# Causal masks added in f32r instead of bf16 in a 24-batch attention and experts kernel

## What is computed

```
# layer 0, "mla":  latent attention, softmax
scores = einsum('bhqd,bhkd->bhqk', q, k) * scale
causal = triu(full((t, t), -inf), k=1)
attn = softmax(scores + causal)
# layer 1, "gqa":  grouped attention, 16 query heads on 4 key heads
scores = where(tril(ones(s, s)), scores, finfo.min);  attn = softmax(scores)
# layer 1, "spm":  the same with sparsemax in softmax's place
scores = where(tril(ones(l, l)), scores, -1e9);       attn = sparsemax(scores)
```

## Time and profile before

| what | value |
|---|---|
| median of 3 runs | 3103.69 us |
| lowest, highest | 3096.67, 3104.48 us |
| the profiled execution's own time | 3129.51 us |
| span in its profile, first to last instruction | 3127.6 us |
| mean granted clock of TensorE in it | 0.956 |
| busy: PE, PEld, DVE, ACT, POOL | 90%, 73%, 68%, 52%, 48% |

### The profile page before, as it was taken

How to read it: one execution, slowest core, us unless ns; L and a number is a source line. 1 busy time by engine, 2 the same in 40 slices (tenths; PEclk the granted TensorE clock), 3 DMA queues, 4 the chain that set the end, 5 groups by cost and what they waited for, 6 DMA issues and landing times. The chain is left out here.

```text
span 3127.6 us, 61182 instructions
## 1 busy us (share of the span) xinstructions
PE 2809.4 (90%) x20990; PEld 2275.6 (73%) x20990; DVE 2133.4 (68%) x6013; ACT 1615.2 (52%) x3388; POOL 1506.6 (48%) x2213
## 2 busy tenths in 40 slices
PE   5877799999999999978998898998799999999996
PEld 3555478888899889846666666666588888888864
DVE  6878678788788788767777877766644444454565
ACT  3544344444454445545655555655455555555553
POOL 4768743443343354385556666322233333332487
PEclk8878799999999999989999999999899999999998
DMA  3555578788888888422333344210466666665355
GB/s 83 197 208 202 196 262 311 278 286 316 284 290 307 294 286 308 178 40 55 97 99 104 105 107 109 93 69 22 164 213 210 228 213 212 204 241 203 124 97 126
DMA packets 212008, 580.13 MB, mean 185 GB/s; under 512 B 24617, under 2 KB 146417, under 8 KB 167409
## 3 DMA queue, kind: packets, MB, share of 16 engines
q1 hardware_dynamic: 172528, 523.82, 47.7%
q0 software_dynamic: 36864, 51.14, 8.1%
q10 hardware_dynamic: 2304, 1.21, 0.1%
HBM read 450.14 MB, written 125.96 MB: 184 GB/s over the span
## 5 line engine op out<-in xcount | busy, mean ns | idle before, releaser
L1139 POOL TENSOR_TENSOR al<-t,ah 128x512 fp32r<-128x512 f32 x220 | 283.4, 1288 | 875.1 <-ACT ah L1375 875.1
L481 PE MATMUL bank<-xh,gu 128*128 128x256 f32 x3520 | 672.3, 291 | 33.6 <-DVE gc L1654 25.8
L481 PEld LDWEIGHTS bank<-xh,gu 128*128 128x128 f32 x3520 | 512.6, 190 | 57.7 <-issue 55.0
L524 PE MATMUL bank<-masks_bf,ident_bf 128*128 128x128 bf16 x1896 | 432.9, 252 | 133.9 <-DVE st L1840 41.0
L1840 DVE TENSOR_REDUCE st<-bank 128x1 f32<-128x512 f32 (+3 forms) x1024 | 422.1, 481 | 166.1 <-PE bank L542 158.6
L1472 ACT ACTIVATE pt<-bank 128x512 f32<-128x512 f32 (+1 forms) x1152 | 512.0, 540 | 30.2 <-PE bank L545 21.9
L524 PEld LDWEIGHTS bank<-masks_bf,ident_bf 128*128 128x128 bf16 x1896 | 170.3, 99 | 353.6 <-DVE st L1840 95.3
L1480 ACT ACTIVATE oT<-bank 128x512 f32<-128x512 f32 x192 | 114.6, 597 | 602.5 <-PE bank L621 576.5
L542 PE MATMUL bank<-ksT,qsT 128*128 128x512 f32 (+3 forms) x1536 | 410.3, 369 | 5.7 <-DVE top L1838 3.1
L545 PE MATMUL bank<-qaT,ksT 128*128 128x512 f32 (+3 forms) x1536 | 399.6, 372 | 0.0
L481 PE MATMUL bank<-xl,gu 128*128 128x256 f32 x1760 | 351.5, 281 | 0.0
(11 more groups left out here) (250 smaller groups left out, 5216.2 us busy)
## 6 DMA issues: line engine op xcount, KB each, us to landing
gu<-wu_scratch SPq DMA_DIRECT2D x110, 1032.0 KB, 5.2
gu<-wu_scratch SPq DMA_DIRECT2D x110, 1024.0 KB, 7.4
dn<-wd_scratch SPq DMA_DIRECT2D x110, 1024.0 KB, 6.7
xs<-xs_scratch SPq DMA_DIRECT2D x110, 264.0 KB, 4.3
ys_scratch<-yb SPq DMA_DIRECT2D x110, 256.0 KB, 7.0
raw<-in_gu SPq DMA_DIRECT2D x16, 1024.0 KB
wu_scratch<-hi SPq DMA_DIRECT2D x16, 1024.0 KB
wu_scratch<-lo SPq DMA_DIRECT2D x16, 1024.0 KB
```

Source lines behind the costliest of these rows:

```text
L481: mm = pe.matmul(bank[:, TS * h:TS * (h + 1)], gu[:, col:col + P], x[s % 2][:, TS * k:TS * (k + 1)], start=(n == 0), stop=(n == len(terms) ...
L524: return pe.matmul(S.bank((which, G, u))[:, diag:diag + P * len(unit)], ident_bf[:, :], masks_bf[:, side, 0:len(unit), :].rearrange("p n k ...
L1139: pool.tensor_tensor(em["al"][s % 2][:, m, :], em["t"][g % 2][:, :], em["ah"][s % 2][:, m, :].bitcast(F32), ALU.subtract).then_inc(al_read ...
```

## The change

Where a mask starts the accumulation, its product is now of f32r: the identity `ident_r` and the triangles `masks_r`, both rounded to f32r once at the start, with the triangle of the unit of two blocks read twice by a broadcast. The operands take 4 bytes an element instead of 2. Where a mask comes last (the q calls within the stretches with experts, and the general pipeline), it stays as it was, with a `masks_bf` that now holds only the triangles of the q side. The masking number becomes minus 2 to the 100th, a power of two, so that rounding leaves it as it is. DVE makes four casts in place of two at the start, and TensorE waits for all four before the first scores. No instruction of TensorE is added, removed or moved.

```
-MASKED = -1.0e30
+MASKED = -2.0 ** 100
...
-    masks_bf = sb("masks_bf", [P, 2, 2, P], BF16)
+    masks_bf = sb("masks_bf", [P, 2, P], BF16)
+    masks_r = sb("masks_r", [P, 2, P], F32R)
+    ident_r = sb("ident_r", [P, P], F32R)
...
-                        return pe.matmul(S.bank((which, G, u))[:, diag:diag + P * len(unit)], ident_bf[:, :],
-                                         masks_bf[:, side, 0:len(unit), :].rearrange("p n k -> p (n k)"),
-                                         start=start, stop=not start, skip_group_check=True)
+                        to = S.bank((which, G, u))[:, diag:diag + P * len(unit)]
+                        if start:
+                            return pe.matmul(to.rearrange("p (n k) -> p n k", k=P), ident_r[:, :],
+                                             bcast(masks_r[:, side, :], 1, len(unit)), start=True, stop=False,
+                                             skip_group_check=True)
+                        return pe.matmul(to, ident_bf[:, :], masks_bf[:, 0:len(unit), :].rearrange("p n k -> p (n k)"),
+                                         start=False, stop=True, skip_group_check=True)
...
-                    pe.wait_ge(cast, 2)
+                    pe.wait_ge(cast, 4)
...
                     dve.tensor_copy(ident_bf[:, :], ident[:, :]).then_inc(cast, 1)
-                    dve.tensor_copy(masks_bf[:, :, :, :], bcast(boot["masks"][:, :, :], 2, 2)).then_inc(cast, 1)
+                    dve.tensor_copy(ident_r[:, :], ident[:, :]).then_inc(cast, 1)
+                    dve.tensor_copy(masks_r[:, :, :], boot["masks"][:, :, :]).then_inc(cast, 1)
+                    dve.tensor_copy(masks_bf[:, :, :], bcast(boot["masks"][:, 0, :], 1, 2)).then_inc(cast, 1)
```

## The result

| | median | lowest to highest | runs |
|---|---|---|---|
| before | 3104.48 us | 3096.67 to 3108.89 | 5 |
| after | 3120.17 us | 3117.42 to 3123.59 | 5 |

The ratio is 1.0057, with a 95% interval of 1.0045 to 1.0069: the changed kernel is slower by 14 to 21 us. That lies within the range of the prediction (3097 to 3124 us), but above its likeliest value by 8.5 us and above the 3106 to 3118 us that it called its forecast, and it is beyond the 0.3% that was called no change.

A forecast was written before the change was run, and what follows sets the result against it. TensorE was taken to mostly set the pace, with gaps in which it waits; only the 124 pairs alone change. Losses of 2 + 4 + 2 = +8 us in their three stretches made 3111.7 us, range 3097 to 3124 us.

The forecast's parts named there:

- The price of the units: Mask units on TensorE: dense k and q triplets 0.98 us, 0.54 us behind outputs, 0.50 us behind a wait.
- The start and the stretches with experts: Two more DVE casts at the start, covered by 1.5 us, cost nothing; the stretches with experts keep their length.
- The k call: Each k call: 0.09 us lost behind the outputs, 0.04 us gained in its other units, together +0.05 us.
- The q call: Each q call: 0.08 us at its last unit, 0.05 at its first, 0.01 in the dense rest, together +0.14 us.
- What lies on the path: Part of the 24 us gross that stays: 2 us in the first stretch, 4 in the middle, 2 in the last.
- I let 1.1 us vanish, 0.4 us stay: Middle stretch, each run of eight pairs: of 1.5 us lost, a 2.7 us wait for DVE swallows 1.1 us.
- Rival (a): All of the loss stays, the wait for DVE swallowing nothing: 16 to 24 us, 3120 to 3128 us; chance 0.18.
- second sign of being wrong: The forecast is wrong if the 124 pairs alone grow by more than 0.13 us or shrink on the mean.
- (b): Rival: the dense k calls' gains win, 7 to 15 us gained, 3089 to 3097 us; chance 0.14.
- (c): Rival: shorter TensorE idling raises its clock, 3101 to 3108 us, down to 3092 us; chance 0.08.
- (d): Rival: the longer f32r loads of all 1488 masks show in full, 153 us, 3257 us; chance 0.02.
- (e): Rival: all is hidden and the edit does nothing measurable, 3104 us; chance 0.08.

The follow-up runs named there:

- e7: f32r masks only in units 1 to 3 (counted from 0) of each k call, all else bf16, against the kernel before: ratio 0.9999.
- second profile: The kernel before, unchanged, run and profiled once more: span 3096.6 us, ratio 0.9997 to the kernel before.
- e9: f32r mask only in the first unit of each q call, all else bf16, against the kernel before: ratio 1.0016.
- e5: f32r masks only in the first and last unit of each q call, all else bf16, against the kernel before: ratio 1.0045.
- e2: f32r masks in all units of the q calls, k calls keep bf16, against the kernel before: 3113.70 us, ratio 1.0042.
- e3: f32r masks in all units of the k calls, q calls keep bf16, against the kernel before: 3111.89 us, ratio 1.0029.
- e4: f32r masks only in the last five units of each k call, all else bf16, against the kernel before: 3106.53 us, ratio 1.0015.
- e10: f32r masks only in the last two units of each k call, all else bf16, against the kernel before: ratio 1.0027.

## Why the prediction was right or wrong

**The price of the units: right.** The dense k triplet measures 0.98 us (forecast 0.98), the q triplet 0.98 us (3051.02 + 0.45 less 3050.49, forecast 0.98), the unit behind the outputs 0.55 us (0.54), the last unit behind its wait 0.49 us (0.50). PEld's busy time grew by 128 us (135). Only the split within a dense triplet was wrong: a mask of 128 columns ends 0.05 to 0.06 us behind the product before it (3045.74 + 0.22 against 3045.45 + 0.46 in the k call shown), not 0.11 us, and the product behind it ends later by as much. In the third unit of the q call it is 0.11 us (3050.68 + 0.27 against 3050.44 + 0.40), in the fourth 0.07 us. By the prediction's own words, which called it wrong under 0.08 us, that step failed in three of the four dense places, though its sum held.

**The start and the stretches with experts: right.** The first projection starts at 15.32 us, again 0.78 us behind ACT as in the earlier trace rows, and the weights were ready at 13.84 us:

```profile
12.94 0.90 DVE L2239 TENSOR_TENSOR w_mla<-f_four,f_bm 128x128 f32<-128x128 f32 x4
...
15.32 2.04 PE L574 MATMUL bank<-w_mla,xT 128*128 128x512 f32 x2 [0.78 <-ACT xT L1422]
```

**The k call: wrong.** The step was "+0.09 - 0.04 (the rest of its units) = +0.05 us". It is +0.15 us in the pair shown, and the same by the medians of the middle stretch's k calls (sixth unit's end 2.13 us behind the outputs before, 2.28 us after). So it cost three times what was forecast. One part of the miss is that the gain of the dense units was counted, though TensorE runs into ACT's release of the bank behind them (e7, 0.9999). The larger part is that the sixth unit, which I took as dense, is behind that release: 0.40 us from its load to its end became 0.49 us, as for any mask behind a wait. Added up along the release it is 0.08 us (the exponentials start later), + 0.09 us (the exposed load), - 0.02 us (the load starts sooner behind its exponential) = 0.15 us. A wait of 0.15 us for `pt` stood before the load of the unit ahead of it in 81 of the middle stretch's 87 calls before (second profile), as a cause of little total time; I had read only the large causes in the earlier trace rows.

**The q call: right in its mechanism.** Where the call waits for keys, the prices forecast make +0.21 us and +0.18 us are measured; the mean of +0.14 us was made with weights, one half for the first unit and four fifths for the last. e9 and e5 give 0.16 and, by difference, 0.29%: about 5 and 9 us, and the forecast had 124 x 0.05 = 6 and 124 x 0.08 = 10 us gross. So they may stay nearly whole, though the intervals are wide and e2 by itself keeps 10.5 of 17 us by its medians.

**What lies on the path: right in kind, mis-sized in the middle stretch.** The first and the last stretch were put at 2 us each and grew by 2.6 and 2.5 us. The middle was put at 4 us and holds nearly all of the rest, some 11 of 15.7 us (15.3 us between the two profiles, clock included). Two terms were off. The price that goes in is 0.15 + 0.14 = 0.29 us a pair and not 0.19 us, so 36 us gross for 124 pairs and not 24 us. And 15.7 / 36 = 44% of it stays, where 8 of 24 us, a third, were forecast.

"I let 1.1 us vanish, 0.4 us stay" can be read in the six batches whose long wait is 2.70 or 2.71 us in the second profile, as in the earlier trace rows. These 48 pairs take 487.2 us before and 491.5 us after, both at a clock of 0.98: 0.7 us stay in each run of eight pairs. Their long wait is 1.29 to 2.64 us after, 0.6 us shorter on the mean (forecast: about 1 us). One of them, in the profile after:

```profile
1940.74 0.38 PE L528 MATMUL bank<-masks_r,ident_r 128*128 128x256 f32 x1 [2.40 <-DVE st L1846]
```

The first 16 pairs of the middle grew by 6.7 us against the second profile, with the clock at 0.89 for 0.93 and then 0.98 for 1.00. Against the first profile, which has 0.89 and 0.98 there too, it is 2.3 us.

Rival (a) has the measured time at the near end of its 3120 to 3128 us, but its mechanism is not what the rows show. It has the wait swallow nothing, and the wait did get shorter. It decides once more than half of the 1.5 us survives a run of eight pairs: in those six batches 0.7 us did, over the whole middle some 11 / 11 = 1.0 us. And "all of it stays" would be 36 us by the prices measured. So the time lies near (a), and still within the range, because a gross price half as large again as forecast met a loss of more than half of it. That is partly luck. The second sign of being wrong, growth of over 0.13 us a pair alone, stands at its edge: 15.7 / 124 = 0.127 us by the medians, 0.17 us by the two profiles.

**The other rivals.** (b) is out: the k calls' gain is real and doesn't reach the time (e7), and e3 is slower. (c) is out as far as two profiles tell: the middle stretch had no higher clock than before (0.96 for 0.97), and the first 0.81 for 0.82. (d) is out: 1488 loads of 0.1 us more are 147 us, and the time grew by 16 us. (e) is out by the interval.

**What stays open.** e4 and e10 should agree and do so only within their intervals, so the loss of the k calls' last two units is 4 to 8 us. Where the 20 us between the gross price and the time vanish is known only in part, by the long wait; which other waits take the rest was not followed pair by pair. The exact share of the middle stretch can't be had from one profile, whose clock differs from execution to execution.

## What to carry to other kernels

Look up what stands at a handover before counting columns or loads in a dense row: a cheaper or dearer product among others changes nothing that can be told here (868 of 1488 masks, 1.0007), while 0.1 us at the first and the last unit of a call shows in the time, here at a little under half of its sum. A load that carries the wait for its bank, or that follows the plain float32 outputs, cost 0.09 to 0.11 us more here, the whole difference of the two loads. So such places are the ones for the operand with the shorter load; in between, either was worth the same here. And a product without idle time before it can still stand behind a release: compare the start of its load with the end of the instruction that frees its bank.

## What was not expected of the hardware

- In a dense row the mask's type hardly matters, though its load is twice as long in f32r and the types no longer alternate: the k triplet takes 1.02 us with bf16 masks and 0.98 us with f32r ones, the q triplet 0.96 us and 0.98 us.
- In a dense row an f32r product of 128 columns mostly ends 0.05 to 0.07 us behind the one before (0.11 us in the third unit of a q call), less than the 0.12 us between ends in the earlier trace rows; the next product ends later by as much. Its load (0.19 us of record) begins 0.10 to 0.19 us after the mask's.
- Behind the last plain float32 output both kinds of load are exposed, and the f32r unit ends 0.11 us later than the bf16 one, much as behind a semaphore (0.09 to 0.10 us). The difference of the two load records is 0.10 us.
- A mask's load can wait for a release while TensorE is busy all the time: in 119 of the changed kernel's 121 k calls behind outputs, the load of the sixth starts 0.03 to 0.10 us after the exponential that frees its bank has ended.
